# Two graph layers in four stages: stage 3 with a load ring of twenty groups and ten x1 rows, in the room of six weight tensors

## What is computed

```
h  = relu(layernorm(x))
L0: agg = zeros.at[dst].add(relu(h[src] + edge_attr)); t = (h + agg) @ W1 + b1     # 256 -> 512
    t = batchnorm over all nodes, relu, @ W2 + b2                                   # 512 -> 256
    t = graph norms over all nodes (one graph): mean and variance, ln_w, ln_b, gn_*
    x1 = x + h + relu(t)
h1 = relu(layernorm(x1))
L1: out = x1 + relu(h1 @ W + segment_sum((h1 @ M)[src], dst))
```

## Time and profile before

| | us |
|---|---|
| median of three runs | 2557.79 |
| lowest and highest run | 2555.56, 2563.54 |
| the profiled execution | 2563.98 |
| its span, first to last instruction | 2562.2 |

### The profile page before, as it was taken

How to read it: one execution, slowest core, us unless ns; L and a number is a source line. 1 busy time by engine, 2 the same in 40 slices (tenths; PEclk the granted TensorE clock), 3 DMA queues, 4 the chain that set the end, 5 groups by cost and what they waited for, 6 DMA issues and landing times. The chain is left out here.

```text
span 2562.2 us, 59007 instructions
## 1 busy us (share of the span) xinstructions
PE 2406.6 (94%) x13809; PEld 2228.8 (87%) x13809; DVE 2144.7 (84%) x6315; ACT 1808.9 (71%) x3908; POOL 1716.1 (67%) x1799
## 2 busy tenths in 40 slices
PE   6899999899999999999999999969999999969897
PEld 5688888699999999999999999958888888858786
DVE  6899999599999999999999999767777777758886
ACT  5799999466666666666666666559888888845554
POOL 5677777466666666666666676347666666737675
PEclk8999999899999999999999999969999999989998
DMA  7999888323444444444444444379999999645553
GB/s 204 243 264 261 261 262 237 93 69 98 156 158 157 156 154 152 152 153 159 159 154 157 152 153 152 113 270 404 381 385 377 374 381 373 242 132 158 157 160 108
DMA packets 310548, 533.61 MB, mean 208 GB/s; under 512 B 74700, under 2 KB 166083, under 8 KB 310454
## 3 DMA queue, kind: packets, MB, share of 16 engines
q1 hardware_dynamic: 250150, 461.89, 53.0%
q0 software_dynamic: 59712, 70.24, 10.3%
q10 hardware_dynamic: 592, 0.54, 0.1%
HBM read 339.38 MB, written 290.19 MB: 246 GB/s over the span
## 5 line engine op out<-in xcount | busy, mean ns | idle before, releaser
L1055 ACT ACTIVATE r<-pair,bnC,bnA 128x384 f32<-128x384 f32 (+1 forms) x524 | 353.2, 674 | 352.7 <-PE pair L1248 352.0
L1008 POOL DMA_INDIRECT ar<-sum_table,idx x391 | 440.3, 1126 | 192.2 <-POOL idx L1004 110.4
L1439 POOL DMA_INDIRECT x1d_table<-x1r,slot x391 | 380.5, 973 | 185.0 <-issue 119.7
L1156 DVE CAST rH<-r 128x384 fp32r<-128x384 f32 (+1 forms) x524 | 393.9, 752 | 43.9 <-ACT r L1055 30.4
L1645 PE MATMUL pair<-Ws,h1T 128*128 128x256 f32 x1564 | 369.4, 386 | 24.0 <-DVE orr L1565 22.1
L1645 PEld LDWEIGHTS pair<-Ws,h1T 128*128 128x128 f32 x1564 | 287.3, 190 | 78.1 <-issue 39.5
L1264 PE MATMUL bank<-rH,W2h 128*128 128x384 f32 x1048 | 352.6, 336 | 1.7 <-ACT yr L1069 1.7
L1264 PE MATMUL bank<-rL,W2h 128*128 128x384 f32 x1048 | 352.4, 336 | 0.0
L1264 PE MATMUL bank<-rH,W2l 128*128 128x384 f32 x1048 | 352.2, 336 | 0.0
L824 PE MATMUL bank<-hr 128*128 128x257 f32 (+1 forms) x1564 | 289.2, 336 | 32.2 <-ACT hr L537 31.7
L1165 DVE TENSOR_TENSOR rL<-r,rH 128x384 fp32r<-128x384 f32 (+1 forms) x524 | 304.0, 580 | 18.0
(11 more groups left out here) (221 smaller groups left out, 5647.9 us busy)
## 6 DMA issues: line engine op xcount, KB each, us to landing
xr<-in_x SPq DMA_DIRECT2D x248, 384.0 KB
x_table<-x1r SPq DMA_DIRECT2D x130, 384.0 KB
out<-orr SPq DMA_DIRECT2D x130, 384.0 KB
xh_table<-xr SPq DMA_DIRECT2D x118, 384.0 KB, 2.3
yT_table<-yr SPq DMA_DIRECT2D x118, 384.0 KB, 2.8
xh_kept<-xh_table SPq DMA_DIRECT2D x86, 384.0 KB, 12.1
y_stays<-yT_table SPq DMA_DIRECT2D x86, 384.0 KB
x1d_table<-blank SPq DMA_DIRECT2D x131, 128.0 KB
```

The lines of the kernel that those rows point to most:

```text
L1008: pool.indirect_dma_start(ar[0:p, s, j, :], None, sum_table[:, :], bass.IndirectOffsetOnAxis(ap=idx[0:p, s, j:j + 1], axis=0), bounds_chec ...
L1055: act.activation(r32[:, m, 0:n], z_ps[m][:, 0:n], ACT.Relu, bias=bnC[:, m:m + 1], scale=bnA[:, m:m + 1]).then_inc(r_kept, 1)
L1156: dve.tensor_copy(rH[:, s, m, 0:n], r32[:, m, 0:n]).then_inc(rh_kept, 1)
L1439: pool.indirect_dma_start(x1d_table[:, :], bass.IndirectOffsetOnAxis(ap=slot[0:p, half, s * T + j:s * T + j + 1], axis=0), x1r[0:p, s, j, ...
```

## The change

The six weight tensors are allocated from the other end of the on-chip memory and are given up before stage 3. Stage 3 takes RL = 20, RU = 10 and LEAD = 18, so that xhr and yr have eight slots each in place of four, and x1r has ten rows in place of eight. POOL's second filling of `slot` follows RU. Since rounds unrolls stage 3 by RL, its bodies have 20 steps in place of 16: on PE, DVE, ACT and POOL the loop runs over five rounds in place of seven, on SP over four in place of six.

```diff
-        def sb(name, shape, dt=FP32, scope=ctx):
-            return scope.enter_context(nc.sbuf_tensor(name, shape, dt))
+        def sb(name, shape, dt=FP32, scope=ctx, side="left"):
+            return scope.enter_context(nc.sbuf_tensor(name, shape, dt, side=side))
+
+        halves = ctx.enter_context(ExitStack())
...
-        W1s = sb("W1s", [P, KC, HID])
-        W2s = sb("W2s", [P, HC, CH])
-        W1h = sb("W1h", [P, KC, HID], FP32R)
...
+        W1s = sb("W1s", [P, KC, HID], scope=halves, side="right")
+        W2s = sb("W2s", [P, HC, CH], scope=halves, side="right")
+        W1h = sb("W1h", [P, KC, HID], FP32R, scope=halves, side="right")
...
+        halves.close()
         next_phase()
         c1 = sem("c1")
...
-        RU = 8
-        RL = 16
+        RU = 10
+        RL = 20
         OL = 4
-        LEAD = 14
+        LEAD = 18
...
                     if u == 3:
                         set_slots(r, 1)
-                    if u == 11:
+                    if u == RU + 3:
                         set_slots(r + 1, 0)
```

More of the change, by code:

```diff
@@ L182, in gnn_kernel @@
         eps = sb("eps", [P, 1])
-        W1s = sb("W1s", [P, KC, HID])
-        W2s = sb("W2s", [P, HC, CH])
-        W1h = sb("W1h", [P, KC, HID], FP32R)
-        W1l = sb("W1l", [P, KC, HID], FP32R)
-        W2h = sb("W2h", [P, HC, CH], FP32R)
-        W2l = sb("W2l", [P, HC, CH], FP32R)
+        W1s = sb("W1s", [P, KC, HID], scope=halves, side="right")
+        W2s = sb("W2s", [P, HC, CH], scope=halves, side="right")
+        W1h = sb("W1h", [P, KC, HID], FP32R, scope=halves, side="right")
+        W1l = sb("W1l", [P, KC, HID], FP32R, scope=halves, side="right")
+        W2h = sb("W2h", [P, HC, CH], FP32R, scope=halves, side="right")
+        W2l = sb("W2l", [P, HC, CH], FP32R, scope=halves, side="right")
         Ws = sb("Ws", [P, KC, CH])
```

## The result

| | before | changed |
|---|---|---|
| median of 11 runs each, us | 2560.94 | 2570.23 |
| lowest and highest run | 2555.56, 2565.62 | 2566.80, 2575.41 |
| ratio, 95% interval | | 1.0034, 1.0022 to 1.0045 |
| profiled execution; span | 2563.98; 2562.2 | 2569.57; 2567.6 |

The change makes the kernel slower, by 0.34%. The forecast was 2556.2 us and its range ended at 2566.0; the time lies outside, on the side that was given one chance in ten.

A forecast was written before the change was run, and what follows sets the result against it. The prediction took stage 3's middle to be bound by DMA bytes and its ends by PE. The ring's -1.6 us and four zero terms took the median from 2557.8 to 2556.2 us, range 2549.5 to 2566.

The forecast's parts named there:

- What bounds the kernel: Stage 3: DMA bytes bound the middle at 4.40 us a group, PE both ends; load ring depth bounds nothing.
- Ring of 20: Stage 3: sixteen loads at the start cost nothing; 18 groups at PE's pace after the last load; net -1.6 us.
- Ten x1 rows: Stage 3: two more x1 rows give nothing, since no x1 sum waits for a store or scatter; 0.
- Room and placement: Weights at the other end, all else 24 KB lower: taken as 0, bounded by the runs' spread, 2555.56 to 2563.54.
- Longer loop bodies: Stage 3: SP stalls 5.4 us at each of three jumps back, DVE not; covered by queued DMA work, cost 0.
- nearly 2 us: Stage 3: SP's second stall at each jump back, for the next instruction piece, after a first of 3.4 us.
- rival 1: Stage 3: SP's fetch stalls are not covered, up to 16.2 us lost, 2572.4 us; chance 8%.
- the 12.2 us from issue to landing: Stage 3: a load's time, taken as about 12 us of queued DMA work that covers SP's 5.4 us stall.
- Rival 2: Stage 3 middle: the ring was the limit, 4.40 falls to 4.00 us a group, -34 us, 2524; chance 2%.
- Rival 3: Stage 4: DVE's body comes to lie in three pieces, its four stalls go, -13.6 us, 2542.6; chance 3%.
- 0.10 for slower: Whole kernel: chance of slowing beyond 0.3%, from uncovered SP stalls at full price or a changed memory order.
- the memory's order: Stage 3 middle: reads 18 groups ahead change bytes per microsecond; 2% for gain, 2% for loss beyond 0.3%.

The follow-up runs named there:

- a_align: Changed kernel with 32 unused bytes a partition beyond the weights, which puts them on multiples of 64; 2559.86 us, ratio 1.0003.
- b_again: The kernel before, unchanged, run once more for a second profile; 2561.63 us.
- b_right: The kernel before with only the six weight tensors allocated from the other end, ring still 16; 2573.19 us, ratio 1.0046.
- e_near64: The kernel before, weights untouched, with a pad of 224 bytes ahead of tH; 2567.26 us in a single execution, stage 2 1167.3 us.
- a_align_sp: a_align with eleven already met waits, each with a no-op, in place of one on SP at the end of stage 2; 2559.57 us, ratio 0.9993.
- a_align_sp_dve: a_align_sp with forty already met waits on DVE ahead of stage 4's rounds; 2549.23 us, ratio 0.9947.
- c_ol8: Kernel before with weights at far end plus 32 bytes, given up before stage 3, forty met DVE waits before stage 4, OL = 8; 2539.27 us, ratio 0.9909.

## Why the prediction was wrong

**What bounds the kernel**: right for stage 3, with a gap. It named stage 3 as "the only stage whose work the change touches" and read no row of stage 2. Stage 2 is 1151 of 2562 us with PE at 200.00 of 200 us. There whatever slows the matmuls by 1% costs 12 us at the end, with nothing to hide it; that could have been read beforehand.

**Ring of 20**: the steps came out as written. Sixteen loads in 8.6 us (7.5 forecast), DMA busy to 1701, 4.0 or less after the last load, 4.40 in the middle with DVE waiting for `out`. The sum of -1.6 us is too small for the totals: a_align gives -0.1 to +0.2% about zero. But all of it was to come at the end of the stage, and there it shows in the profiles. From the x1 sum of group 110 to that of group 124 the four kernels with the ring of 16 and OL = 4 (before, b_again, b_right, e_near64) take 58.4 to 59.1 us, the five with the ring of 20 and OL = 4 on these chips 56.9 to 57.5, which is 1.6 us less on average. The changed kernel's -6.2 us of stage 3 is not the ring's gain: a_align has 550.5 us with the same ring, and with the old one b_right has 545.0 and e_near64 541.7. Executions of one and the same stage 3 spread by some 5 us (548.9 in a_align_sp, 543.4 in a_align_sp_dve); up to 2 us of such a spread is the moment at which the clock comes back.

**Ten x1 rows**: 0, and no run contradicts it; POOL's wait for scatters is 2.4 us against 3.0.

**Room and placement: the step that failed.** "No row prices an address; I take 0, bounded by the spread of the runs shown." Measured on its own in b_right: 13.6 us (2573.19 against 2559.58). It was bounded by the spread of one program's runs, and such a spread says nothing on what another program does: all runs of one kernel have the same addresses. What no row prices should have been bounded by what the stage lets through: stage 2 has PE without a gap, so any slowing of its matmuls arrives whole, 12 us for 1%. That it would be about 1% could not be read beforehand; that the range needed such a term could. The mechanism itself, groups of matmuls at 176.7 ns in place of 173.3, stays open. The Trainium skill (SBUF — State Buffer, "Operand start alignment") asks only that an operand start at a multiple of its element size. All placements here do, and 32 bytes still cost or save 13 us; the page gives no price for a place.

**Longer loop bodies**: SP stalls at the three jumps back that were named, and DVE doesn't. The size was wrong: 5.4 us was forecast and it is 6.3 + 4.1 = 10.4. The first part was read in stage 4, where the DMA engines are half busy, and the "nearly 2 us" of the second stood on no row. That the fetches take longer because the DMA engines are full in stage 3 is likely but argued; the prediction named it as a reason for rival 1 and didn't put it into the sum. The cost at the end was right, 0, but its cover was not the one given, and the 0 is in so far luck: the 12.2 us from issue to landing did not stand for 12 us of queued work, since the share fell to 0.80 with a first pause of 6.3 us, and a higher rate afterwards made it good. a_align against a_align_sp shows the zero.

**The rivals.** Rival 1 gave 2572.4 us, which is near the time measured, by coincidence: the pauses came and the DMA share dropped, as it said, but with the pauses removed nothing is gained. Rival 2 is refuted, the middle stays at 4.40. Rival 3's mechanism is real: it did not occur in the changed kernel (13.4 us in four stalls, as before), and made to occur in a_align_sp_dve it gives 10 us of its 13.6.

**The chances**: 0.10 for slower held only rival 1 and the memory's order. A mechanism without a row had got no chance of its own.

## What to carry to other kernels

Where an engine is busy without a gap for a whole stage, a change of placement elsewhere can be a change of that stage: count its instructions in a fixed stretch before and after (1206 against 1191 here), since busy shares and slices show nothing, and try a pad of 32 bytes before believing any other explanation. Then look at the spacing group by group: an average of 175.6 hid groups at 173.3 and at 176.7, and with them the fact that the addresses were the same in both. An instruction stall costs what its engine lacks in slack in that stage, so the same mechanism was worth 10 us on DVE in stage 4 and nothing on SP in stage 3, although longer there. And when a stage is bound by the DMA engines at its middle and by compute at its ends, spare room can do more in the ring that drains (c_ol8, 0.9909) than in the one that fills; here it did.

## What was not expected of the hardware

- TensorE's spacing of 128x384 fp32r matmuls has two levels, 173.3 and 176.7 ns, at the same granted clock of 1.00. It holds one of them for a whole group of 48 behind six transposes and changes between groups that use the same addresses; the placement of tensors decides how many groups are slow (85 in the changed kernel, one before). The rule is open.
- A fetch of loop code takes 3.4 to 4.0 us of DVE's time with the DMA engines half busy, and 10.4 us of SP's in two pauses where they are full.
- The DMA engines move 393 to 408 GB/s after a pause (and 400 in 1733 to 1813 of the kernel before, without one) and 372 to 378 in the undisturbed middle, at shares of 1.00 to 1.03. A share of 1 is thus not yet the most that they can move.
